# Gated FFN stage: integers transposed as 16-bit halves, GpSimd takes every second rounding and every fourth product, two banks for the down sums

## The reference

```python
def _act_quant(x):
    scale = 127.0 / jnp.clip(jnp.max(jnp.abs(x), axis=-1, keepdims=True), 1e-05)
    xq = jnp.clip(jnp.round(x * scale), -128.0, 127.0) / scale
    return x + jax.lax.stop_gradient(xq - x)
def _bitlinear(x, w):
    return jnp.einsum('bsi,oi->bso', _act_quant(x), _weight_quant(w))
gate = jax.nn.silu(_bitlinear(x, w_gate))
up = _bitlinear(x, w_up)
return _bitlinear(gate * up, w_down)
...
x = x + jnp.tanh(g_ffn[0]) * _L0_ffn_ref(_layernorm(x, axis=-1), L0_ffn_w_gate, L0_ffn_w_up, L0_ffn_w_down)
```

## Time and profile before

| | before |
|---|---|
| median of 3 runs | 1501.96 us (1485.5 to 1505.27) |
| the profiled execution | 1501.73 us, its span 1499.7 us |
| PE busy | 1339.9 us (89%) |
| DVE busy | 1170.0 us (78%) |
| ACT busy | 1063.8 us (71%) |
| POOL busy | 762.5 us (51%) |

### The profile page before, as it was taken

The page is one execution under the profiler, slowest core; times in us unless marked ns, Lnnn a source line. Parts: engine busy times, 40 slices in busy tenths (PEclk is TensorE's granted clock), DMA queues, the critical chain, the costliest instruction groups (busy, mean ns, idle before and its releaser), DMA issues.

```text
span 1499.7 us, 30709 instructions
## 1 busy us (share of the span) xinstructions
PE 1339.9 (89%) x11525; PEld 910.6 (61%) x11580; DVE 1170.0 (78%) x1896; ACT 1063.8 (71%) x1795; POOL 762.5 (51%) x1206
## 2 busy tenths in 40 slices
PE   4799999999999999999987999999789888177697
PEld 2566666666666666666653666666667666143385
DVE  4447788788878888877777999988447899878896
ACT  2346777777777777777755888888545666689996
...
GB/s 163 116 72 80 129 131 99 143 126 116 112 132 133 102 149 107 108 116 115 74 92 1 1 2 1 1 1 1 103 158 141 90 162 106 1 235 354 28 400 386
DMA packets 125603, 171.99 MB, mean 115 GB/s; under 512 B 47490, under 2 KB 78338, under 8 KB 120066
## 3 DMA queue, kind: packets, MB, share of 16 engines
...
q10 hardware_dynamic: 288, 0.00, 0.0%
...
## 4 chain that ended last, share of the span: by engine, by line
PE 65%; ACT 11%; DVE 11%; DMA 5%; issue 3%; POOL 3%; SPq 2%; DVEq 0%; POOLq 0%; ACTq 0%
PE psum L557 10%; PE psum L568 10%; PE psum L544 7%; PE psum L585 5%; PE psum L532 5%; PE psum L602 4%; ACT f_gelu L1964 4%; PE psum L943 3%; PE psum L969 3%; PE psum L961 3%; ACT f_gelu L1973 3%; PE psum L506 3%; DMA f_gelu<-g_scratch 2%; PE psum L519 2%; PE psum L1399 2%
## 5 line engine op out<-in xcount | busy, mean ns | idle before, releaser
L735 DVE TENSOR_REDUCE neg_max<-psum 128x8 f32<-128x1024 f32 x256 | 313.2, 1224 | 78.0 <-PE psum L544 73.5
L672 ACT ACTIVATE exp_t<-psum 128x512 f32<-128x512 f32 x512 | 281.6, 597 | 55.6 <-PE psum L557 55.4
L838 POOL TENSOR_TENSOR rs<-rs,minus_half 128x16 f32<-128x16 f32 x64 | 186.7, 2918 | 5.0
L557 PEld LDWEIGHTS psum<-q_stack,k_stack 50*128 50x128 f32 x2048 | 140.4, 195 | 80.3 <-issue 77.9
L557 PE MATMUL psum<-q_stack,k_stack 50*128 50x128 f32 x2048 | 177.0, 294 | 0.3 <-ACT exp_t L672 0.2
L568 PE MATMUL psum<-exp_t,v_pad 128*32 128x256 f32 x2048 | 171.4, 408 | 0.0
L677 ACT ACTIVATE o_t<-psum 128x512 f32<-128x512 f32 x128 | 76.5, 598 | 102.1 <-PE psum L568 101.8
L544 PE MATMUL psum<-k_stack,q_stack 48*128 48x256 f32 x1024 | 138.2, 350 | 6.7 <-DVE neg_max L735 6.2
L830 POOL TENSOR_TENSOR sq<-u 128x256 f32<-128x256 f32 x64 | 39.2, 612 | 190.9 <-DVE u L752 190.3
L943 PE MATMUL psum<-f_w,f_xqt 128*128 128x512 bf16 x481 | 118.3, 386 | 6.5 <-DVE f_hid L1071 3.8
L544 PEld LDWEIGHTS psum<-k_stack,q_stack 48*128 48x128 f32 x1024 | 84.1, 196 | 56.9 <-issue 45.4
...
## 6 DMA issues: line engine op xcount, KB each, us to landing
k_stack<-k_hi SPq DMA_DIRECT2D x256, 128.0 KB, 4.7
g_scratch<-f_gelu SPq DMA_DIRECT2D x21, 1024.0 KB, 3.9
f_gelu<-g_scratch SPq DMA_DIRECT2D x21, 1024.0 KB, 14.8
k_stack<-k_lo SPq DMA_DIRECT2D x128, 128.0 KB, 4.8
...
```

The costliest lines, as they stand in the source:

```text
L557: r = e.matmul(psum[:, 2 + j, o:o + P], self.k_st[rows, b // 2 % self.NK, pair // 2 % 2, pair % 2, i, pair // 4, b % 2, :], self.q_st[rows ...
L672: e.activation(self.prob[:, n % 3, j].rearrange("p n w t -> p (n w t)"), psum[:, 2 + j, :], ACT.Exp).then_inc(s["exp"], 1)
L735: e.tensor_reduce(self.negm[:, b % 2, :, :, 2 * u:2 * u + 2].rearrange("p j w n -> p j n w"), psum[:, 0:2, :].rearrange("p j (n w k) -> p ...
L838: e.tensor_tensor(self.rs[:, i], self.rs[:, i], self.expo[:, :], ALU.pow).then_inc(s["pool"], 1)
```

## The change

- `quantise` and `requantise` add LOW = ROUND + 2^14 instead of ROUND. The low 16 bits of the fp32 number then hold integer + 16384. `low` views these halves as bf16 with a step of two elements. PE transposes them with a bf16 identity (`ident16`, made by one POOL copy at the start), and ACT reads the PSUM result as int16 and subtracts 16384.
- `turn_x(j)` turns two tiles at once, in even steps, directly after `gate_up`; `x_turned(j)` copies both in one instruction, in odd steps, ahead of `h_turned`. `xqt` holds 4 tiles.
- A transposed hidden tile fills one bank (4). `down` alternates between banks 5 and 7 and waits for `add(b - 2)`.
- For b = 4, 8, ..., 56 (14 tiles) the product leaves DVE: ACT copies the scaled up sums to `hid` (`up_copied`), POOL multiplies by silu (`product`, in POOL step b + 2).
- For odd b from 5 to 59 (28 tiles) the hidden tile is rounded by POOL (`requantise`, in POOL step b + 7) instead of by ACT.
- DVE's `add` goes ahead of the maxima where tile b - 1 was POOL's, and hidden_max(b - 1), hidden_max(b) follow it.
- POOL's `finish` moves from steps 8k + 1 to 8k + 3. `Ffn1.NSEM` is 6.

The core of the diff:

```diff
     H, NHT, HS = 1024, 8, 8
+    BASE = 2.0 ** 14
+    LOW = ROUND + BASE
     XR = 4
...
-        self.xqt = sb("f0_xqt", [P, 2, 2, P], BF16)
+        self.xqt = sb("f0_xqt", [P, 4, 2, P], BF16)
         self.gact = sb("f0_act", [P, 2, self.H])
-        sb("f0_rest", [P, 528])
+        self.ident16 = sb("f0_ident16", [P, P], BF16)
+        sb("f0_rest", [P, 528 - 256 - 64])
...
+    def low(self, ap):
+        return ap.bitcast(BF16).rearrange("p (n two) -> p n two", two=2)[:, :, 0]
+    def product_on_pool(self, b):
+        return b % 4 == 0 and 4 <= b < NSEQ - 4
+    def rounded_on_pool(self, b):
+        return b % 2 == 1 and 4 <= b < NSEQ - 4
...
+    def up_read(self, w, n):
+        on_pool = sum(self.product_on_pool(b) for b in range(n))
+        w.wait_ge(self.s["up_sb"], on_pool)
+        w.wait_ge(self.s["hid"], n - on_pool)
...
+    def hr_made(self, w, n):
+        on_pool = sum(self.rounded_on_pool(b) for b in range(n))
+        w.wait_ge(self.s["hr_pool"], on_pool)
+        w.wait_ge(self.s["hr"], n - on_pool)
...
-        def turn_x(b):
+        def turn_x(j):
             w.wait_ge(a0.s["m_sb"], NSEQ)
-            w.wait_ge(s["xr"], b + 1)
-            w.wait_ge(s["xt_sb"], b)
-            for h in range(2):
-                r = e.transpose(psum[:, 6, h * P:(h + 1) * P], self.xr[:, b % self.XR, h * P:(h + 1) * P], sh.ident[:, :])
+            w.wait_ge(sh.s["made"], 5)
+            w.wait_ge(s["xr"], 2 * j + 2)
+            w.wait_ge(s["xt_sb"], j - 1)
+            out = psum[:, 6, j % 2 * 256:j % 2 * 256 + 256].bitcast(BF16)
+            for i in range(2):
+                for h in range(2):
+                    r = e.transpose(out[:, (2 * i + h) * P:(2 * i + h + 1) * P],
+                                    self.low(self.xr[:, (2 * j + i) % self.XR, h * P:(h + 1) * P]), self.ident16[:, :])
             r.then_inc(s["xt_pe"], 1)
...
-            w.wait_ge(s["hid"], b)
+            self.up_read(w, b)
...
             w.wait_ge(a0.s["x_new"], NSEQ)
-            w.wait_ge(s["hr"], b + 1)
+            self.hr_made(w, b + 1)
             w.wait_ge(s["ht_sb"], b)
+            out = psum[:, 4, :].bitcast(BF16)
             for i in range(self.NHT):
-                r = e.transpose(psum[:, 4 + i // 4, i % 4 * P:(i % 4 + 1) * P], self.hr[:, b % 2, i * P:(i + 1) * P], sh.ident[:, :])
+                r = e.transpose(out[:, i * P:(i + 1) * P], self.low(self.hr[:, b % 2, i * P:(i + 1) * P]), self.ident16[:, :])
             r.then_inc(s["ht_pe"], 1)
...
             tw.wait_ready(w, 2)
-            w.wait_ge(s["x_new"], b)
+            w.wait_ge(s["x_new"], b - 1)
             for n in range(self.NHT):
-                r = e.matmul(psum[:, 7, 0:D], self.hqt[:, b % 2, n, :], wd[:, n, :], start=n == 0, stop=n == self.NHT - 1)
+                r = e.matmul(psum[:, 5 + 2 * (b % 2), 0:D], self.hqt[:, b % 2, n, :], wd[:, n, :], start=n == 0, stop=n == self.NHT - 1)
...
+            if b % 2 == 0 and 0 <= b + 2 < NSEQ:
+                turn_x((b + 2) // 2)
             if 0 <= b - 7 < NSEQ:
                 down(b - 7)
-            if 0 <= b + 2 < NSEQ:
-                turn_x(b + 2)
...
+        def x_turned(j):
+            i = 2 * j % 4
+            w.wait_ge(s["xt_pe"], j + 1)
+            w.wait_ge(s["up_pe"], 2 * j - 2)
+            e.activation(self.xqt[:, i:i + 2].rearrange("p b h t -> p (b h t)"),
+                         psum[:, 6, j % 2 * 256:j % 2 * 256 + 256].bitcast(mybir.dt.int16), ACT.Copy, bias=-self.BASE).then_inc(s["xt_sb"], 1)
...
+        def up_copied(b):
+            w.wait_ge(s["up_pe"], b + 1)
+            self.hr_made(w, b - self.HS + 1)
+            e.activation(self.hid[:, b % self.HS], psum[:, 2:4, :].rearrange("p j c -> p (j c)"), ACT.Copy,
+                         scale=self.s_up[:, b:b + 1]).then_inc(s["up_sb"], 1)
...
             e.activation(self.hr[:, b % 2], self.hid[:, b % self.HS], ACT.Copy, scale=self.hscale[:, b:b + 1],
-                         bias=ROUND).then_inc(s["hr"], 1)
+                         bias=self.LOW).then_inc(s["hr"], 1)
...
-            e.activation(self.hqt[:, b % 2].rearrange("p n t -> p (n t)"), psum[:, 4:6, :].rearrange("p j c -> p (j c)"), ACT.Copy,
-                         bias=-ROUND).then_inc(s["ht_sb"], 1)
+            e.activation(self.hqt[:, b % 2].rearrange("p n t -> p (n t)"), psum[:, 4, :].bitcast(mybir.dt.int16), ACT.Copy,
+                         bias=-self.BASE).then_inc(s["ht_sb"], 1)
...
+            if b % 2 and 0 <= b + 1 < NSEQ:
+                x_turned((b + 1) // 2)
             if 0 <= b - 7 < NSEQ:
                 h_turned(b - 7)
             if 0 <= b < NSEQ:
                 silu(b)
-            if 0 <= b - 5 < NSEQ:
+                if self.product_on_pool(b):
+                    up_copied(b)
+            if 0 <= b - 5 < NSEQ and not self.rounded_on_pool(b - 5):
                 requantise(b - 5)
-            if 0 <= b + 2 < NSEQ:
...
         def step(b):
             if 0 <= b < NSEQ:
-                hidden(b)
-                hidden_max(b)
+                if not self.product_on_pool(b):
+                    hidden(b)
+                if not self.product_on_pool(b) and not self.product_on_pool(b - 1):
+                    hidden_max(b)
+            if 0 <= b - 7 < NSEQ:
+                add(b - 7)
+            if 0 <= b < NSEQ:
+                if self.product_on_pool(b - 1):
+                    hidden_max(b - 1)
+                    hidden_max(b)
                 if b % 4 == 3:
                     hidden_scale(b // 4)
-            if 0 <= b - 7 < NSEQ:
-                add(b - 7)
...
-            w.wait_ge(s["xt_pe"], b - self.XR + 1)
-            e.tensor_scalar(self.xr[:, b % self.XR], self.xn[:, b % 16], self.qscale[:, b:b + 1], ROUND, ALU.mult, ALU.add).then_inc(s["xr"], 1)
+            w.wait_ge(s["xt_pe"], (b - self.XR) // 2 + 1)
+            e.tensor_scalar(self.xr[:, b % self.XR], self.xn[:, b % 16], self.qscale[:, b:b + 1], self.LOW, ALU.mult, ALU.add).then_inc(s["xr"], 1)
+        def product(b):
+            w.wait_ge(s["silu"], b + 1)
+            w.wait_ge(s["up_sb"], sum(self.product_on_pool(i) for i in range(b + 1)))
+            h = self.hid[:, b % self.HS]
+            e.tensor_tensor(h, h, self.gact[:, b % 2], ALU.mult).then_inc(s["hid_pool"], 1)
+        def requantise(b):
+            w.wait_ge(s["h_scale"], self.HSCALE * (b // 4 + 1))
+            w.wait_ge(s["ht_pe"], b - 1)
+            e.tensor_scalar(self.hr[:, b % 2], self.hid[:, b % self.HS], self.hscale[:, b:b + 1], self.LOW, ALU.mult, ALU.add).then_inc(s["hr_pool"], 1)
...
+            if b == -16:
+                w.wait_ge(sh.s["const_loaded"], 16)
+                e.tensor_copy(self.ident16[:, :], sh.ident[:, :]).then_inc(sh.s["made"], 1)
             if 0 <= b + 4 < NSEQ:
                 quantise(b + 4)
+            if 0 <= b - 2 < NSEQ and self.product_on_pool(b - 2):
+                product(b - 2)
+            if 0 <= b - 7 < NSEQ and self.rounded_on_pool(b - 7):
+                requantise(b - 7)
             if b % 4 == 1 and 0 <= b - 5 < NSEQ:
                 hidden_scale((b - 5) // 4)
             if b == 10:
                 sh.finish(w, 1, NSEQ // 8 - 1)
-            if b % 8 == 1 and b >= 17:
-                sh.finish(w, 2, (b - 17) // 8)
+            if b % 8 == 3 and b >= 19:
+                sh.finish(w, 2, (b - 19) // 8)
...
-    NOUT, SLOTS, NSEM = OUT // 2, RING // 2, 8
+    NOUT, SLOTS, NSEM = OUT // 2, RING // 2, 6
```

25 lines of the change are left out of this document (12 added, 13 removed).

## The result

| | before | changed |
|---|---|---|
| median | 1487.3 us (20 runs, 1476.7 to 1505.27) | 1495.22 us (20 runs, 1487.05 to 1516.68) |
| changed / before | | 1.0048, 95% interval 1.0025 to 1.007 |
| the profiled execution, its span | 1501.73, 1499.7 us | 1488.9, 1486.8 us |
| gated FFN stage, first `hidden` to last `add` | 268.3 us | 277.5 us |
| eight tiles in its middle (P) | 30.97 us | 34.2 to 34.8 us |

A ratio is taken from fast runs alone (those within some 1.5% of the fastest run of their kernel), so it is not the quotient of two medians, which cover all runs.

A forecast was written before the change was run, and what follows sets the result against it. PE and DVE were taken as near their limit, with room on POOL. Six periods of 33.7 against 30.98 us gave +16.3, the end -4, the start 0: +12.3 on 1501.73, so 1514 us, range 1494 to 1532.

The forecast's parts named there:

- The queue on POOL: POOL steps 8k + 1 and 8k + 2: product and rounding stand behind the reciprocal wait, a 4.6 us stall per eight tiles.
- the clock's 1.4: PE after its 5.3 us idle time: slower turn_h and gate at the lowered clock cost 1.4 us, taken as 1.2.
- One sign of the prediction: In the changed profile, POOL's wait for DVE's reciprocal would be nearly gone (the queue arrives late) or short.
- P: Eight tiles mid-stage: DVE 26.7, stall 4.6, other waits 1.2, clock 1.2, making 33.7 us against 30.98.
- The transposes: PE: each bf16 transpose 0.08 us, between 0.055 and 0.109, cutting PE's work for eight tiles from 29.5 to 27.2.
- the end: Tiles 56 on and drain: one product less, shorter transposes (2.3 us) and seven shorter turn_h (1.6 us), -4 us.
- the bank: Second down bank: removes PE's wait for add, 0.8 us in eight tiles, but nothing extra counted as DVE paces PE too.
- The base: Whole kernel: the profiled execution of 1501.73 us, within 0.3 us of the median, to which +12.3 was added.
- Lateness is hidden: Rival, gated FFN stage: POOL's lateness costs nothing, eight tiles about 28.3 us, -20 in all, 1482 us; chance 0.15.
- The transposes are faster: Denies the rival on PE that transposes are no faster: eight tiles 36 us, +30, 1532 us; chance 0.12.
- the product is not dear: Denies the rival that POOL's product takes over 3 us, each us more adding 6; 1521 us at 3.5; chance 0.08.
- Nothing moves outside the stage: Outside the gated FFN stage: the prediction would be wrong if anything moved there.

The follow-up runs named there:

- The experiment that only moves the wait: Changed kernel with POOL's token scales and their reciprocal wait moved from the head of step 8k + 1 to the end of 8k + 2: 1471.01 us, ratio 0.9844.
- the rounding alone: Changed kernel with every product back on DVE, POOL still rounding every second hidden tile: 1495.27 us, ratio 1.0029.
- the transposes alone: Changed kernel without product or rounding on POOL; 16-bit transposes, paired copies, two down banks and later finish remain: 1458.2 us, ratio 0.9758; on another chip 1462.82 us, 0.9813.
- the rounding one step earlier: Changed kernel with POOL's token scales moved to step 8k + 2 and its rounding issued at t + 6 instead of t + 7: 1471.84 us, ratio 0.9788.
- the best order: Changed kernel, POOL rounding one step earlier, DVE's small clamp moved behind step 8k + 1's maxima, POOL's token scales moved to 8k + 3: 1456.49 us, ratio 0.9807.

## Why the prediction was right and wrong

**The queue on POOL: right, nearly to the tenth.** Counted from the `add` of step 8k (875.07), predicted and read: POOL wakes at 2.13 and 2.14; the product starts at 4.8 and 4.80 and ends at 7.2 and 7.14; the rounding is done at 8.3 and 8.24; PE goes on at 8.4 and 8.30 after 5.3 and 5.29 us; `hidden(8k + 2)` starts at 11.3, with the clock's 1.4 at 12.7, and 12.84. The experiment that only moves the wait shows that this chain carries the loss, and the one with the rounding alone that its second job is enough for it. One sign of the prediction did not come: POOL's wait for the reciprocal is neither nearly gone nor short (7.16 us here). The chain starts late because the reciprocal is late, and not because POOL is.

**P: 33.7 predicted, 34.2 to 34.8 read.** The product (2.4, measured 2.35) and the rounding (1.1, measured 1.12) were right. DVE's own work without the two products was taken as 26.7; over the four periods from tile 17 to 49 DVE is busy 104.92 of 137.73 us, 26.2 in each. The clock was taken as 1.2 and is worth 2.0 to 2.5. The six stretches came to +15.9 where I had +16.3: the first, 9 to 17, is only 29.65 us, since tile 3 is not rounded by POOL, which I had counted as a full one, and the other five came out some 3.6 us longer in all than I had them. Two errors of some 4 us cancelled there, which is luck.

**The transposes: 0.08 taken, 0.056 measured.** Eight bf16 transposes run from 891.92 to 892.37, 0.45 us or 0.056 each, half of the 0.109 of the fp32 ones; the lower bound. In the trace of the transposes alone PE is busy 25.7 us in eight tiles, near the 25.2 of that bound. The Trainium skill, "TensorE: Matmul & The Clock Gate", Back-to-back issue gap, gives about 81 ns for the sustained stream of weight load and 128-column matmul and 56 for one by itself; here the stream itself has the second. In the middle that is hidden under the stall. At the end it is not: from tile 57 on the stage wins 7.6 us, and I had 4 (2.3 and 1.6; the product less, which I named, is not in that sum). In the drain a tile takes 2.61 us now; PE's rows there wait 1.12 us for ACT:

```profile
1036.03 1.05 PE L1011 MATMUL psum<-f_w_down,f_hqt 128*128 128x256 bf16 x8 [1.12 <-ACT f_hqt L1072]
1036.92 0.61 PE L1003 MATMUL psum<-f_ident,f_hr 128*128 128x128 bf16 x8
1038.64 1.05 PE L1011 MATMUL psum<-f_w_down,f_hqt 128*128 128x256 bf16 x8 [1.12 <-ACT f_hqt L1072]
```

and none of them waits for `add` as in the earlier trace rows, nor runs at the lower clock. The second bank takes that wait away; whether it is also what keeps the clock up is not shown, since in the experiment with one bank PE waits 1.75 us at this place and its granted clock stays at 1.00. I had counted nothing for the bank; its own experiment puts 6 to 8 us on it, where POOL does no product and no rounding.

**The sum: +12.3 predicted for the stage, +9.2 read**, and 1.0048 x 1487.3 makes +7.1 in the runs. Term by term the middle had +16.3 and came to +15.9, the end had -4 and came to -7.6, the start had 0 and came to +1.0. The term that was wrong in the stage is the end.

**The base: the step that failed.** "The profiled execution of 1501.73, which is within 0.3 us of the median" was true of three runs and said little: they lay at 1485.5, 1501.96 and 1505.27, and I took their middle for the kernel's level. What stands in its place is 1487.3, the median of 20 runs. The 22 us by which the changed kernel reaches the stage earlier have nothing to do with the change. Stretches from the start, of the kernel before and then of the changed one:

```profile
50.00:70.00 20.00, 18.02 (x115) 12.42 (x112) 10.05 (x13) 10.03 (x19) 2.51 (x7) 0.50 0.85 145
70.00:120.00 50.00, 49.78 (x297) 31.86 (x295) 23.45 (x38) 22.15 (x43) 14.62 (x20) 0.50 0.29 55
```

```profile
50.00:70.00 20.00, 18.02 (x119) 12.46 (x119) 10.27 (x14) 10.03 (x19) 2.29 (x7) 0.50 0.85 146
70.00:120.00 50.00, 49.31 (x495) 32.62 (x491) 38.31 (x63) 37.13 (x74) 29.49 (x45) 0.98 0.61 103
```

Both have PE busy all the time from 70 to 120 us, before at 0.50 with 297 matmuls, after at 0.98 with 495. The profiled execution of the kernel before with six semaphores, whose stage is the same, has 0.98 and 495 there too; it reaches the stage at 775.5 us and takes 1484.92 instead of 1501.73. It is no property of the kernels, since two executions of one and the same kernel, the transposes alone, differ in the same way. First the one that reaches the stage at 778.0 us, then the one at 795.6:

```profile
70.00:120.00 50.00, 49.31 (x461) 32.59 (x459) 36.36 (x59) 34.27 (x69) 28.85 (x45) 0.90 0.60 103
```

```profile
70.00:120.00 50.00, 49.78 (x293) 32.42 (x290) 22.68 (x37) 23.04 (x45) 15.25 (x22) 0.50 0.29 55
```

The time less the stage says the same: the medians of the kernel before, of the changed one and of the two with the transposes alone and with the clamp moved, less their stages, are 1219.0, 1217.7, 1215.8 and 1216.8 us. Of the 18.8 us between 1514 and the measured median, then, 14.4 are the base and 3.1 the stage; the remaining 1.3 lie between medians and single executions. A stretch at 0.50 with PE busy could have been read in the profiled execution beforehand, as a reason to doubt the middle of three runs that lie 20 us apart; I read only the stage. That 1495.22 lies inside the range of 1494 to 1532 at all is chance: its low end was there for a stall that is partly hidden, and this one was not.

**The rivals.** "Lateness is hidden" did not come; its time, 20 us off the base, is about what came once the wait stood behind the work (the stage at 250.4, 17.9 us under that of before), so the reason that I gave against it, the place of the reciprocal in the queue, was the right one. The transposes are faster, the product is not dear. "Nothing moves outside the stage" held between these two traces, but for the clock of the first 120 us. That the stretch behind the stage came out alike, 434.1 and 434.0 us, is chance as well: over all the traces of this case it is 434.0 to 448.3 us, 438.0 for the kernel before with six semaphores. In the trace where it is longest, that of the rounding one step earlier, the granted clock is low there while PE is busy: 0.50 from 1219 to 1234 us with PE busy all the time.

What stays open: why P is 27.2 and not DVE's 25.7 (102.80 of the 108.88 us of four periods) in the best order; what lets the clock at the start come up early in some executions and late in others, and fall behind the stage; and whether the small clamps would be held up by any POOL work or by products alone, for which no experiment was made. The trace of the best order hints at any POOL work: its 4-column clamps (0.16 us alone) take 0.23 to 0.26 where a rounding on POOL ends beside them, and end with it. Against that stands one such clamp in the trace of the rounding alone, which kept its 0.16 us beside a `normalise`.
